# Last layer of a two-layer network: six put-away base tiles kept in SBUF, routing rows copied out before the expert table, x1 tiles in the weight space, last tile finished by column halves

## The reference, cut to what matters

```python
y = einsum('bij,bkj->bik', x1, weight[adapter_ids])      # one of 16 adapters per batch
base = einsum('bsi,oi->bso', y, base_w) + base_b         # dense, 1024 x 1024
hidden = einsum('bsi,ri->bsr', y, A)                     # 64 features per token
probs = softmax(einsum('bsi,ei->bse', y, router_w))      # 16 experts, the best two used
delta = einsum('bse,bsr,eor->bso', combine, hidden, B)   # each token's two experts
out = x1 + base + delta * 0.5
```

## Time and profile before

| | |
|---|---|
| time, median of 3 runs | 1214.57 us (1213.8 to 1217.22) |
| the profiled execution's own time | 1211.74 us |
| its span, first to last instruction | 1210.1 us |
| PE busy | 1115.4 us, 92% of the span |
| DVE busy | 689.7 us, 57% |
| ACT busy | 504.9 us, 42% |
| POOL busy | 221.0 us, 18% |
| DMA traffic | 289.38 MB, mean 239 GB/s |
| mean TensorE clock granted | 0.977 of full |

### The profile page before, as it was taken

One profiled execution on the slowest core, in us unless ns is written; L12 is line 12 of the kernel. 1 busy time (PEld: TensorE's weight loads), 2 busy tenths in 40 slices (PEclk: granted clock), 3 DMA queues, 4 the chain that ended last, 5 costly groups with the idle time before them and its releaser, 6 DMA issues.

```text
span 1210.1 us, 22388 instructions
## 1 busy us (share of the span) xinstructions
PE 1115.4 (92%) x5799; PEld 921.9 (76%) x5800; DVE 689.7 (57%) x1307; ACT 504.9 (42%) x1019; POOL 221.0 (18%) x352
## 2 busy tenths in 40 slices
PE   4989969988999899999999899989999899999997
PEld 4979958867888677777887778767676678888885
DVE  2877863472554728364555386735444366666655
ACT  1101213562654638363556471134444344444443
POOL 1021110020110202010111000054444042323220
PEclk8989979998999999999999999999999999999998
DMA  5488764493573828475665333169999799999995
GB/s 203 162 325 279 268 237 128 129 319 129 183 267 105 323 77 306 134 250 193 215 222 189 124 98 104 64 220 363 369 351 282 280 377 353 341 355 336 358 344 202
DMA packets 115051, 289.38 MB, mean 239 GB/s; under 512 B 17202, under 2 KB 21810, under 8 KB 112946
## 3 DMA queue, kind: packets, MB, share of 16 engines
q1 hardware_dynamic: 85088, 184.91, 42.9%
q0 software_dynamic: 29056, 102.38, 25.5%
q10 hardware_dynamic: 850, 1.39, 0.4%
HBM read 184.79 MB, written 103.84 MB: 239 GB/s over the span
## 4 chain that ended last, share of the span: by engine, by line
PE 65%; DVE 13%; DMA 9%; issue 7%; ACT 3%; SPq 2%; DVEq 1%; ACTq 1%; another core or an unknown queue 0%; POOLq 0%; POOL 0%
PE psum L1344 14%; PE psum L1346 14%; PE psum L1345 14%; PE psum L1529 3%; PE psum L1428 3%; DMA delta_scratch<-dl 2%; PE psum L1530 2%; PE psum L1420 2%; PE psum L1538 2%; PE psum L1355 2%; PE psum L1446 2%; DMA xp<-act_scratch 2%; PE psum L1448 2%; DMA rawb<-baseT 2%; DVE x1g L985 2%
## 5 line engine op out<-in xcount | busy, mean ns | idle before, releaser
L1344 PE MATMUL psum<-base_hi,xp_hi 128*128 128x512 f32 x512 | 204.2, 399 | 2.5 <-ACT nat L757 1.5
L1344 PE MATMUL psum<-w,xp_hi 128*128 128x512 f32 x448 | 185.5, 414 | 19.8 <-DVE xp_lo L1035 17.2
L1345 PE MATMUL psum<-base_lo,xp_hi 128*128 128x512 f32 x512 | 200.8, 392 | 0.0
L1346 PE MATMUL psum<-base_hi,xp_lo 128*128 128x512 f32 x512 | 200.7, 392 | 0.0
L1346 PE MATMUL psum<-w,xp_lo 128*128 128x512 f32 x448 | 180.0, 402 | 0.0
L1345 PE MATMUL psum<-w,xp_hi 128*128 128x512 f32 x448 | 179.8, 401 | 0.0
L583 POOL DMA_DIRECT2D raw<-w1T x112 | 59.3, 529 | 461.8 <-DVE w L1014 461.3
L1014 DVE TENSOR_TENSOR w<-raw,w 128x1024 fp32r<-128x1024 f32 x112 | 132.1, 1218 | 5.5 <-ACT w L696 3.5
L749 ACT ACTIVATE xp_hi<-xp 128x256 fp32r<-128x256 f32 x124 | 51.4, 416 | 179.4 <-PE psum L1346 137.8
L1116 DVE TENSOR_TENSOR xp_lo<-xp,xp_hi 128x256 fp32r<-128x256 f32 x124 | 51.9, 424 | 117.9 <-ACT xp_hi L749 95.2
L1344 PEld LDWEIGHTS psum<-w,xp_hi 128*128 128x128 f32 x448 | 85.7, 191 | 42.6 <-issue 24.8
(11 more groups left out here) (263 smaller groups left out, 1912.6 us busy)
## 6 DMA issues: line engine op xcount, KB each, us to landing
raw<-w1T POOLq DMA_DIRECT2D x120, 512.0 KB, 5.6
delta_scratch<-dl SPq DMA_DIRECT2D x80, 512.0 KB
xp<-act_scratch SPq DMA_DIRECT2D x74, 256.0 KB, 2.8
act_scratch<-yT SPq DMA_DIRECT2D x72, 256.0 KB, 4.7
xg<-xT SPq DMA_DIRECT2D x16, 1024.0 KB, 7.4
act_scratch<-x1g SPq DMA_DIRECT2D x16, 1024.0 KB, 5.1
x1t<-act_scratch SPq DMA_DIRECT2D x64, 256.0 KB
out<-x1t SPq DMA_DIRECT2D x64, 256.0 KB
```

The lines of the kernel that those rows point to most:

```text
L1344: mm(out, a_hi, b_hi, start=start, stop=False, skip_group_check=True)
L1345: mm(out, a_hi, b_lo, start=False, stop=False, skip_group_check=True)
L1346: return mm(out, a_lo, b_hi, start=False, stop=stop, skip_group_check=True)
```

## The change

Four things are changed in the last layer.

1. Of the 13 put-away base tiles only tiles 0 to 6 (`FAR = 7`) go to DRAM and back. Tiles 7 to 10 are copied by ACT to four new SBUF buffers `held`, and tiles 11 and 12 stay in the two `nat` buffers; DVE adds straight from there.
2. The x1 buffers move to the expert weights' space and `held` takes their old place. So the first four x1 tiles can be loaded only after the last expert product; SP issues them then, in turn with the put-away tiles' loads.
3. `expert_table` is made after the fifth `row_of_rows`, not after the eighth, so that nothing stands between the eighth and the copy of `rows`. The first pair's transposes, `hw_high(0)` and `hw_low(0)` go among the last steps of tile 7. The register load of the expert number for s + 1 goes ahead of the base step of s.
4. The last tile (31) multiplies the first column half through all eight chunks, then the second. DVE, PE and SP finish it by halves, with four stores of 128 KB in place of two of 256 KB.

```diff
+HELD = 4
+FAR = KEPT - HELD - 2
@@ buffers
+            x1t = [...]            # now beside ga, gb and fin, in the expert weights' space
-            x1t = [sb(s, f"x1t{i}", [P, 2, KC, C]) for i in range(FRING)]
+            held = [sb(s, f"held{i}", [P, D]) for i in range(HELD)]
+        def kept_home(t):
+            return held[t - FAR] if FAR <= t < FAR + HELD else nat[t % 2]
@@ SP
-                keep(t)
+                if t < FAR:
+                    keep(t)
-                    if n == 3 and t > FIRST:
-                        keep(t - 1)
-                if s % 8 == 5 and s // 8 < FRING:
-                    load_x1(s // 8)
-            keep(KEPT - 1)
             sp.wait_ge(x_done, 2 * NX)
             for f in range(FRING):
                 load_kept(f)                     # now only for t < FAR
+                load_x1(f)
@@ SP, store_out
+                if f == NT - 1:
+                    for q in range(2):
+                        sp.wait_ge(out_ready, 2 * f + q + 1)
+                        for h in range(2):
+                            sp.dma_start(out[... q * 256:(q + 1) * 256 ...], x1t[f % FRING][:, h, ks, :] ...)
+                    return
@@ ACT, tile 7's last steps
                     y_high(t, q)
+                    if t == FIRST and q == 2:
+                        hw_high(0)
@@ DVE
                 row_of_rows(n)
+                if n == 4:
+                    expert_table()
-            expert_table()
             dve.tensor_copy(rows[:, :], bank(7)[:, 0:NX]).then_inc(rows_done, 1)
-            for q in range(4):
+            for q in range(3):
                 y_low(8, q)
             hw_low(0)
+            y_low(8, 3)
@@ DVE, add_experts
+                    if t < FAR: base = fin[a][:, :]          # after the load has landed
+                    else:       base = kept_home(t)[:, :]
+                elif t == NT - 1:                             # per column half h
+                        dve.wait_ge(y_used, 4 * t + 2 * h + 2)
+                        dve.scalar_tensor_tensor(out=fin[a][:, hs], in0=ga[a][:, hs], ...)
+                        dve.scalar_tensor_tensor(out=fin[a][:, hs], in0=gb[a][:, hs], ...)
@@ PE
-                k, h = n // 2, n % 2
+                k, h = (n % KC, n // KC) if t == NT - 1 else (n // 2, n % 2)
+                    if t == FIRST - 1 and n == 12:
+                        turn_hw(0)
-            turn_hw(0)
+            e = expert_of(0)
             for s in range(NX):
-                expert(s)
+                expert(s, e)
+                if s + 1 < NX:
+                    e = expert_of(s + 1)
                 for t, n in mixed(s):
                     base_part(t, n)
@@ PE, turn_out
+                    if f == NT - 1 and i == KC // 2:
+                        pe.wait_ge(n2_done, NT + 1)
```

More of the change, by code:

```diff
@@ L94, in build @@
     dls = nc.dram_tensor("delta_scratch", (NX * P, D), F32, kind="Internal").ap()
-    bas = nc.dram_tensor("base_scratch", (KEPT, P, D), F32, kind="Internal").ap()
+    bas = nc.dram_tensor("base_scratch", (FAR, P, D), F32, kind="Internal").ap()
     ctx = ExitStack()
@@ L109, in build @@
             fin = [sb(s, f"fin{i}", [P, D]) for i in range(FRING)]
+            x1t = [sb(s, f"x1t{i}", [P, 2, KC, C]) for i in range(FRING)]
         w = sb(ctx, "w", [P, 2, KC, D], F32R)
@@ L491, in load_kept @@
                 t = ORDER[f]
-                if t < KEPT:
+                if t < FAR:
                     if f >= FRING:
@@ L495, in load_kept @@
                     for a in range(2):
-                        sp.wait_ge(kept_out[a], 16 * ((KEPT + 1 - a) // 2))
+                        sp.wait_ge(kept_out[a], 16 * ((FAR + 1 - a) // 2))
                     sp.dma_start(fin[f % FRING][:, :], bas[t, :, :]).then_inc(fin_in[f % FRING], 16)
@@ L500, in store_out @@
                 t = ORDER[f]
+                if f == NT - 1:
+                    for q in range(2):
+                        ks = slice(q * KC // 2, (q + 1) * KC // 2)
+                        sp.wait_ge(out_ready, 2 * f + q + 1)
+                        for h in range(2):
+                            sp.dma_start(
+                                out[bass.ds(batch_of(t, h), 1), :, q * 256:(q + 1) * 256].rearrange("b p r -> p (b r)"),
+                                x1t[f % FRING][:, h, ks, :].rearrange("p i c -> p (i c)")
+                            ).then_inc(out_stored[f % FRING], 16)
+                    return
                 sp.wait_ge(out_ready, 2 * f + 2)
@@ L520, in _ @@
             for a in range(FRING):
-                sp.wait_ge(out_stored[a], 32 * (NT // FRING))
+                sp.wait_ge(out_stored[a], 32 * (NT // FRING + a // (FRING - 1)))
         @block.gpsimd
@@ L753, in keep @@
                 act.wait_ge(y_used, 4 * t + 4)
-                if t >= 2:
-                    act.wait_ge(kept_out[t % 2], 16 * (t // 2))
+                home = kept_home(t)
+                if home is nat[t % 2] and t >= 2:
+                    act.wait_ge(kept_out[t % 2], 16 * min(t // 2, (FAR + 1 - t % 2) // 2))
                 for h in range(2):
-                    act.activation(nat[t % 2][:, h * 512:(h + 1) * 512], bank(3 + 2 * (t % 2) + h), ACT.Copy
+                    act.activation(home[:, h * 512:(h + 1) * 512], bank(3 + 2 * (t % 2) + h), ACT.Copy
                                    ).then_inc(kept_done, 1)
@@ L793, in _ @@
                     act.activation(rv[:, 4, :], rv[:, 2, :], ACT.Exp).then_inc(exp1, 1)
-            hw_high(0)
             for s in range(NX):
@@ L1274, in add_experts @@
                 if t < KEPT:
-                    dve.wait_ge(fin_in[a], 16 * sum(ORDER[i] < KEPT for i in range(a, f + 1, FRING)))
-                    dve.scalar_tensor_tensor(out=fin[a][:, :], in0=ga[a][:, :], scalar=g1[:, t:t + 1], in1=fin[a][:, :],
+                    if t < FAR:
+                        dve.wait_ge(fin_in[a], 16 * sum(ORDER[i] < FAR for i in range(a, f + 1, FRING)))
+                        base = fin[a][:, :]
+                    else:
+                        dve.wait_ge(kept_done, 2 * t + 2)
+                        if f >= FRING:
+                            dve.wait_ge(ft_done, 2 * (f - FRING) + 2)
+                        base = kept_home(t)[:, :]
+                    dve.scalar_tensor_tensor(out=fin[a][:, :], in0=ga[a][:, :], scalar=g1[:, t:t + 1], in1=base,
                                              op0=ALU.mult, op1=ALU.add).then_inc(n1_done, 1)
                     dve.wait_ge(n1_done, sum(i < KEPT for i in ORDER[:f + 1]))
+                elif t == NT - 1:
+                    dve.wait_ge(ft_done, 2 * (f - FRING) + 2)
+                    for h in range(2):
+                        hs = slice(h * 512, (h + 1) * 512)
+                        dve.wait_ge(y_used, 4 * t + 2 * h + 2)
+                        dve.scalar_tensor_tensor(out=fin[a][:, hs], in0=ga[a][:, hs], scalar=g1[:, t:t + 1],
+                                                 in1=bank(3 + 2 * (t % 2) + h), op0=ALU.mult, op1=ALU.add
+                                                 ).then_inc(base_taken, 1)
+                        dve.wait_ge(base_taken, 2 * (t - KEPT) + h + 1)
+                        dve.scalar_tensor_tensor(out=fin[a][:, hs], in0=gb[a][:, hs], scalar=g2[:, t:t + 1],
+                                                 in1=fin[a][:, hs], op0=ALU.mult, op1=ALU.add).then_inc(n2_done, 1)
+                    return
                 else:
@@ L1481, in base_part @@
                         pe.wait_ge(xp_lo_done, total * 2 + n // 8 + 1)
-                elif n % 4 == 0:
-                    pe.wait_ge(yl_done, 4 * t - 3 + n // 4)
+                elif h == 0 and k % 2 == 0:
+                    pe.wait_ge(yl_done, 4 * t - 3 + k // 2)
                 hs = slice(h * 512, (h + 1) * 512)
@@ L1520, in turn_hw, with expert_of, expert @@
                 last.then_inc(hwT_done, 1)
-            def expert(s):
-                e = pe.value_load(etab[0:1, s:s + 1], min_val=0, max_val=E1 - 1)
+            def expert_of(s):
+                return pe.value_load(etab[0:1, s:s + 1], min_val=0, max_val=E1 - 1)
+            def expert(s, e):
                 pe.wait_ge(hwl_done, s // 2 + 1)
```

## The result

The change made the kernel slower by 0.71%: 1222.64 us median (1221.42 to 1224.28, 5 runs) against 1216.42 (1213.8 to 1217.32, 5 runs), ratio 1.0071 [1.0045, 1.0096]. The forecast was 1210.9, range 1205.5 to 1215.0; "slower" had 0.07. The profiled execution took 1221.42 us with a span of 1219.8 and a mean granted clock of 0.967 (before 1211.74, 1210.1, 0.977).

The account below looks back on a forecast made before the run. PE sets the pace, transfers close behind, so saved traffic counts only through PE's waits. Routing +0.6, clock 0, mixed stage -2.0, later last stage -0.8, end -1.5 give -3.7: 1214.57 to 1210.9 us, range 1205.5 to 1215.0.

Parts of the forecast that it names:

- Start of last stage: First transposes of the last stage: y load goes out at about 970.6, cover over 6 us; 0 us, between -1.8 and +6.0.
- slower rival: Start of last stage: moved x1 loads delay the first gathers by up to 6.0 us; +3.6, 1218.2 us; chance 0.07.
- Routing: Tile 6 to the experts: new 2.75 us wait, +2.7, and the 2.09 us wait gone, -2.1; sum +0.6 us.
- The step for the clock: Slow clock before the third product goes, 1.3 us, the same charged after the pause at 777: 0, bounds +1.7 and -1.3.
- free routing: Tile 6: DVE has slack enough, so PE loses nothing; -2.7 more, 1208.2 us; chance 0.10.
- Mixed stage: Expert and base products together: less traffic gives -0.6 and shorter late waits -1.4; -2.0 us, between 0 and -8.
- the unnamed wait: Fourth expert product 1.89 us late at 804.77, DVE and ACT waiting for something unnamed; kept in the sum, could be -1.9.
- the late waits: PE waits 7.4 us in five pieces from 932.9 to 947.4, caused by the last gathers, which stay; -1.4 us.
- more is freed: Unnamed wait gone, -1.9, and late episode loses half of its 7.4 us, -2.3 more: -7.9, 1206.7 us; chance 0.19.
- The register load's 0: Earlier load of the expert number on PE's sequencer is worth 0 us, bounds 0 and -12.
- The end: After the last base matmul: last store goes out 1.2 us earlier and is half as long; -1.5 us, bounds 0 and -2.6.

Follow-up runs that it names:

- experiment 1: Changed kernel, but SP issues tile 15's y load ahead of the first put-away and x1 loads: 1210.52 us, ratio 1.003 to the kernel before.
- experiment 2: Kernel before with only parts 1 and 2 of the change (kept tiles on chip, x1 buffers moved): 1215.27 us, ratio 1.0056.
- experiment 3: Kernel before with parts 1 and 2 of the change, and tile 15's y load issued ahead of the x1 loads: 1211.32 us, ratio 0.9985.
- experiment 4: Changed kernel, y load still late, but in tile 14 ACT biases and DVE finishes both waiting tiles before touching tile 15's y: 1207.75 us, ratio 1.0003.
- experiment 5: Kernel before with only the expert table made after the fifth eighth instead of the eighth: 1212.94 us, ratio 1.0041.
- experiment 7: Changed kernel with tile 15's y load first and the expert table made after the copy of the rows: 1201.97 us, ratio 0.994 to the kernel before.
- experiment 10: Changed kernel with tile 15's y load first, the table after the row copy, and empty slots reading their own partition's row: 1199.01 us, ratio 0.9878 to before.
- experiment 11: Kernel before with end by halves, first pair early, table after row copy, spread padding rows; no parking, x1 loads unmoved: 1199.79 us, ratio 0.9887.
- experiment 6: Kernel before with only the first pair's transposes, high and low parts in tile 7's last steps: 1206.15 us, ratio 0.9978.
- experiment 8: Kernel before with only the last tile by column halves: 1207.67 us, ratio 0.9993.
- experiment 9: Kernel before with empty slots gathering the row numbered by their partition instead of row 0: 1202.2 us, ratio 0.995.

## Why the prediction was wrong

**The step that failed is "Start of last stage".** It saw the y load go out late, by 4 us (it was 6.7), and put its cost at nothing because it "was needed only for tile 15, which PE starts about 982". That is true of the data and false of the lists. ACT's and DVE's first steps on tile 15's y stand between the finishing of tile 13 and that of tile 0, and PE wants tile 0's transposes at step 9 of tile 14, about 981.7. From the landing to the start of the additions went 0.8 us (987.1 to 987.89), the additions took 2.6: for no wait at 981.7 the load had to land by 978.3. A landing at 987.1 is 8.8 us beyond it, and the wait was 8.88. In the trace of before the same sum, from the second transposes at 980.8, gives 977.4, and the load landed at 975.6: the cover was 1.8 us, not over 6, and even the forecast delay of 4 us would have used it up. The landing itself was mis-sized too. The load went out at 973.3 and not at 970.6: SP began with the x1 tiles at 963.4 and not at 961, of which 1.9 us are the later start of tile 13 in this trace, and the loads ahead took 9.9 us for 9.6. Then the y load needed 13.8 us instead of 9.0, beside the x1 tiles and the gathers. Experiments 1, 2 and 3 show that the place of this load is the whole loss of the stage (240.4 and 239.3 us with the load first, 247.6 and 248.6 with it behind, 239.7 before), and experiment 4 that the order behind it makes it so. The working asked what the load is needed for, not what stands behind its waiting instruction.

**The slower rival was right in its cause and wrong in its place.** It priced the x1 loads at up to +6 us, but on the gathers and so on the first transposes; those waited 0.61 us. Its argument against ("SP can issue 2 MB no faster than in 8.8 us") was the very reason for the late y load.

**Routing.** The step gave a wait of 2.75 us at 776.8 and the 2.09 us wait gone: measured 2.51 and gone, in the profile +2.0 us with a clock of 0.50 from about 777.8 to 781. The step for the clock, 0 with bounds of 1.7, was too small. The same wait of 2.5 us left the clock at 1.00 in experiment 1's trace and at 0.50 for 13 us in experiment 5's. The runs say what the table's place costs in the mean: 0.41% alone (experiment 5), and 0.9% between experiments 1 and 7, where the wait itself is 0.21%. Why the second figure is twice the first stays open. A slow clock behind the wait fits the rest, though it wasn't measured apart: over the 12 runs of experiment 1 the mean granted clock falls as the time rises, from 0.977 in the fastest to 0.968 in the slowest, with a median of 0.9715 against 0.9775 in experiment 7. I estimate that 0.006 of 1205 us, lost by running at 0.50 in place of 1.00, is about 7 us. Where in those runs the clock was low is not on record. The copy of the rows came 12.3 us after the fifth eighth (784.11), and 11.95 before (786.39 in the earlier trace rows), so it was not 0.8 us earlier as forecast: it waits for PE's eighth group, and PE was late. The rival "free routing" is refuted by the wait of 2.51.

**Mixed stage.** -2.0 was forecast. The profile has +2.5, of which 1.5 lie before the fourth product, at the unnamed wait and a slower clock. That wait is in the traces of before and after and, with 0.6 to 2.8 us on ACT or DVE, in those of experiments 3, 10 and 11, which share a chip, and in none of the eight from the other two chips. So it isn't the change's, and what it is stays open. The remaining 1.0 us comes in small steps before the late waits. These were 4.44 us in one piece for 6.9 in five, but behind the one long wait the clock fell to 0.50 (943 to 946), and from the gather at 911.07 (before) or 912.76 (after) to tile 13 both took 49 us. (The prediction's 7.4 for the five pieces holds the 0.56 at 851.6 a second time, and its 210 GB/s is 223 in the window of the earlier trace rows; neither enters its sum.) So "more is freed" fell.

Where the unnamed wait is absent, first expert product to tile 13 took, with the first pair early, 161.2, 161.7 and 161.7 us with parking (experiments 1, 4 and 7) and 162.6 without (experiment 6); with the old pair, 163.3 with parking (experiment 2) and 163.9 without (experiment 8), but 166.3 in experiment 5 (and 167.6 with parking in experiment 3, where the wait is present). Like for like that is a gain of about 1 us where 2.0 was forecast, within what single traces differ by. The cause given for the late waits, the last gathers and not the stores, was right: experiment 9 took the stage to 157.1 us by the gathers' addresses alone, 5.5 less than experiment 6 on the same chip.

**The rest.** The register load's 0 wasn't tried alone and stays open. The end was forecast at -1.5: the trace has -1.1 (8.8 alone in experiment 8, against 10.2). Four stores took 3.98 us of issue from 1213.98; the first went out 1.4 us after the two last additions began (1212.56), SP's issue being last as said.

**The sum.** Alone, the parts gave +0.56% (parking), +0.41% (table), -0.22% (pair) and -0.07% (end), together +0.68%, 8.3 us; the change gave +0.71%. So the parts account for the loss. That they meet it so closely is luck: the four intervals together leave an uncertainty of about 0.4%, 5 us, and experiment 1 gave back less than the parts say.

## What to carry to other kernels

A transfer's cover ends where the first in-order list reaches the instruction that waits for it, not where its data is used: for each load that a change delays, walk from its waiter down each list and ask which other engine needs the next entry. Issue what the next compute step needs ahead of bulk prefetches, above all where the queues are full. Taking traffic off a stage is worth only the waits it ends; 4.2 MB less was worth about 1 us here, which can't be told from nothing, while other addresses for the padding reads (2048 of 10240 slots) were worth 6.

## What was not expected of the hardware

Gathers of many equal rows slowed both queues. With every padding slot at row 0, 0.30 MB took 29.6% of the engines' time in 18 us (0.51 MB 50.2%), with different rows 0.30 MB took 4.3%, and the whole kernel gained 0.50% [0.34, 0.66]. SP's queue moved 6.24 MB in the window (experiment 9) instead of 4.41 (experiment 6). The Trainium skill (DMA: Bandwidth & Descriptors, section Queues, rings and completion order) says that an engine takes turns among its queues packet by packet. By that rule one queue's slow packets hold up the other queue, and the 6.24 MB for 4.41 agree with it. What makes a repeated row slow was not measured.

The granted clock after one and the same pause of 2.5 us of PE was 1.00 in two traces (experiments 1 and 4), 0.50 for about 3 us in that of after, and 0.50 for 13 us in that of experiment 5, of kernels whose work is the same up to there. With the pause, experiment 1's 12 runs lay between 1203.95 and 1216.04 us, and the profiled one was the fastest; without it, experiment 7's 6 runs lay between 1200.25 and 1205.89. The price of such a pause can't be read from a single trace.
